# Slot scatters ordered one slot later, from a ring of four output buffers

## The reference

```python
x = x + gnn(layernorm(x), adj)       # quantised weights and activations, relu, adj @ support
xn = layernorm(x)
probs = softmax(xn @ Wr + br); top 2 of 16 experts per row, weights renormalised
h = gelu(layernorm(xn @ W1[e] + b1[e]) * g1[e] + be1[e])
y = x + sum over the row's 2 experts of weight * (h @ W2[e] + b2[e])
```

## Time and profile before

| what | us |
|---|---|
| median of 3 runs | 493.76 |
| the runs | 492.7 to 495.56 |
| the profiled execution | 493.86 |
| its span in the profile | 492.1 |
| PE busy | 454.0 (92%) |
| DVE busy | 350.0 (71%) |
| ACT busy | 306.0 (62%) |
| POOL busy | 228.2 (46%) |

### The profile page before, as it was taken

The page is one execution under the profiler, slowest core; times in us unless marked ns, Lnnn a source line. Parts: engine busy times, 40 slices in busy tenths (PEclk is TensorE's granted clock), DMA queues, the critical chain, the costliest instruction groups (busy, mean ns, idle before and its releaser), DMA issues.

```text
span 492.1 us, 10312 instructions
## 1 busy us (share of the span) xinstructions
PE 454.0 (92%) x2260; PEld 373.2 (76%) x2261; DVE 350.0 (71%) x735; ACT 306.0 (62%) x511; POOL 228.2 (46%) x267
## 2 busy tenths in 40 slices
PE   0789999999999999989999999999899998999990
PEld 0568888877888888868777888888787776888870
DVE  5898864786788877876757686677896775767730
ACT  1667462474544334346878778779886975897550
POOL 4363330342155627553455655454535636455542
PEclk9999999999999999899999999999999999999997
DMA  8621224885645644249969787966889788675543
GB/s 303 266 79 51 87 65 172 297 313 171 227 156 178 206 137 130 85 116 276 282 173 257 210 246 199 252 134 206 258 239 302 234 218 259 164 193 87 87 67 43
DMA packets 33532, 91.30 MB, mean 186 GB/s; under 512 B 6160, under 2 KB 6304, under 8 KB 32992
## 3 DMA queue, kind: packets, MB, share of 16 engines
q1 hardware_dynamic: 19664, 60.60, 37.6%
q0 software_dynamic: 9232, 21.98, 21.0%
q10 hardware_dynamic: 4608, 8.39, 4.6%
HBM read 71.89 MB, written 19.07 MB: 185 GB/s over the span
## 4 chain that ended last, share of the span: by engine, by line
PE 60%; DMA 14%; DVE 8%; issue 6%; ACT 3%; DVEq 2%; POOL 2%; SPq 1%; POOLq 1%; ACTq 1%
PE ps L1595 18%; PE ps L1854 7%; PE ps L1858 7%; PE ps L1850 7%; PE ps L1579 6%; DMA w_raw<-in_w 6%; DMA out<-y_sb,scat_i 5%; PE ps L1567 5%; PE ps L1635 2%; PE ps L1760 2%; PE ps L1874 2%; DVE w_split L1460 1%; PE ps L1626 1%; DMA gw_raw<-in_gnn_w 1%; PE ps L1555 1%
## 5 line engine op out<-in xcount | busy, mean ns | idle before, releaser
L776 POOL DMA_INDIRECT out<-y_sb,scat_i x35 | 63.0, 1799 | 43.2 <-DMA out<-y_sb,scat_i 25.7
L1460 DVE TENSOR_TENSOR w_split<-w_raw,w_split x56 | 67.2, 1221 | 11.1 <-issue 10.4
L747 POOL DMA_INDIRECT xg<-xn_rows,tok_i x39 | 45.4, 1164 | 46.4 <-ACT gate L972 31.7
L1021 ACT ACTIVATE g_sb<-ps,be_sb,g_sb 128x128 f32<-128x128 f32 x152 | 56.9, 455 | 15.8 <-PE ps L1874 15.6
L832 ACT ACTIVATE adj_hi<-adj_raw,small 128x1024 fp32r<-128x1024 f32 x32 | 36.8, 1150 | 40.6 <-PE ps L1595 34.5
L1007 ACT ACTIVATE w_split<-w_raw x28 | 53.0, 1912 | 5.9 <-DMA w_raw<-in_w 4.9
L1153 DVE SCALAR_TENSOR_TENSOR adj_lo<-adj_raw,small,adj_hi 128x1024 fp32r<-128x1024 f32 x32 | 40.8, 1276 | 19.7 <-ACT adj_hi L832 19.6
L1483 DVE TENSOR_SCALAR h_hat<-ps,h_mv,h_rs 128x512 f32<-128x512 f32 x38 | 30.7, 809 | 26.2 <-POOL h_rs L758 26.1
L1595 PE MATMUL ps<-sup,adj_lo 128*128 128x512 f32 x192 | 49.2, 398 | 0.0
L1595 PE MATMUL ps<-sup,adj_hi 128*128 128x512 f32 x192 | 49.2, 398 | 0.0
L1850 PE MATMUL ps<-w_split,gt_hi 128*128 x152 | 44.5, 414 | 0.7 <-ACT gt_hi L1026 0.7
(11 more groups left out here) (220 smaller groups left out, 952.6 us busy)
## 6 DMA issues: line engine op xcount, KB each, us to landing
w_raw<-in_w SPq DMA_DIRECT2D x64, 512.0 KB
adj_raw<-in_adj_steps SPq DMA_DIRECT2D x32, 512.0 KB, 3.5
out<-x_sb ACTq DMA_DIRECT2D x16, 256.0 KB, 2.8
xn_rows<-xn ACTq DMA_DIRECT2D x16, 256.0 KB, 2.8
bias_rows<-in_b SPq DMA_DIRECT2D x16, 256.0 KB
x_sb<-in_x SPq DMA_DIRECT2D x3, 1024.0 KB, 12.3
gw_raw<-in_gnn_w SPq DMA_DIRECT2D x1, 1024.0 KB, 4.9
x_sb<-in_x SPq DMA_DIRECT2D x2, 512.0 KB, 6.7
```

Source lines behind the costliest of these rows:

```text
L747: return pool.indirect_dma_start(to, None, xn_rows, bass.IndirectOffsetOnAxis(ap=tok_i[:, s:s + 1], axis=0)).then_inc(landed[s % 2], 16)
L776: pool.indirect_dma_start(out, bass.IndirectOffsetOnAxis(ap=at, axis=0), y_sb[:, par, :], None, compute_op=ALU.add).then_inc(scattered[par ...
L1021: ins = act.activation(g_sb[:, par, c * P:(c + 1) * P], ht_ps(par)[:, c * P:(c + 1) * P], ACT.Gelu, scale=g1_sb[:, bass.ds(e * C + c, 1)], ...
L1460: return dve.tensor_tensor(w_parts(n, 1, e + 1, 2 * h, 2), w_raw[:, n, :, :].rearrange("p a n -> p (a n)")[:, at], w_parts(n, 0, e + 1, 2 ...
```

## The change

In `pool_pair`, iteration s now orders the scatter of slot s - 2 instead of s - 1. The first scatter moves from ahead of the loop into it. In the last pair that runs (rest == j) one more scatter, of slot 2j, is ordered at the end, so that again three are left for `give_last`. The gated copies go to a ring of four buffers (`y_ring`, slot modulo 4), and those of the last three slots to three buffers of their own (`y_last`), for which ACT waits for no scatter. Both lie in space that the graph layer used before. The dump rows are written by four DMAs instead of two, so that each parity's semaphore begins at 32 instead of 16; all waits on the scatters are renumbered with it. In the loop ACT's wait has the same number as before and so now means the scatter of slot s - 5 instead of s - 3, where s is the slot whose iteration makes the copy of s - 1.

```diff
--- before.py
+++ after.py
@@ -302,12 +302,16 @@
         g_sb = place("g_sb", [P, 2, D], F32)
         gt_hi = place("gt_hi", [P, 2, D], F32R)
         gt_lo = place("gt_lo", [P, 2, D], F32R)
-        y_sb = place("y_sb", [P, 2, D], F32)
         idx_s = place("idx_s", [P, 3], I32)
         h_stats = place("h_stats", [P, 2, 6], F32)
         h_mv = place("h_mv", [P, 2, 2], F32)
         h_rs = place("h_rs", [P, 2, 4], F32)
         assert where[0] <= end_sup
+
+        where[0] = end_sup
+        y_ring = place("y_ring", [P, 4, D], F32)
+        y_last = place("y_last", [P, 3, D], F32)
+        assert where[0] <= w_at
 
         where[0] = raw_at
         hit_row0 = place("hit_row0", [P, 2 * TQ, P], F32R)
@@ -644,9 +648,9 @@
                     pool.memset(bias_row1[:, :].bitcast(F32), 0.0).then_inc(bias_zero, 1)
             pool.wait_ge(tables_in, 16)
 
-            for h in range(2):
-                pool.dma_start(out[N + h * P // 2:N + (h + 1) * P // 2, :], k_sb[h * P // 2:(h + 1) * P // 2, 0:D]
-                               ).then_inc(scattered[h], 16)
+            for h in range(4):
+                pool.dma_start(out[N + h * P // 4:N + (h + 1) * P // 4, :], k_sb[h * P // 4:(h + 1) * P // 4, 0:D]
+                               ).then_inc(scattered[h % 2], 16)
 
             for dst, name in ((tri_r, "tri"), (ones_r, "ones"), (ident_r, "ident"), (first_r, "first_rank"),
                               (word_r, "word_of")):
@@ -771,18 +775,18 @@
                 pool.wait_ge(gate_ok, s + 4)
                 gather(s + 5)
 
-            def add_rows(at, par):
+            def add_rows(at, rows, par):
                 pool.sem_inc(pool_turn, 1)
                 pool.indirect_dma_start(
                     out, bass.IndirectOffsetOnAxis(ap=at, axis=0),
-                    y_sb[:, par, :], None, compute_op=ALU.add).then_inc(scattered[par], 16)
+                    rows, None, compute_op=ALU.add).then_inc(scattered[par], 16)
 
             def give(s, start):
 
-                pool.wait_ge(scattered[s % 2], s // 2 * 16 + 16)
-                pool.wait_ge(scattered[1 - s % 2], start * 16 + (s + 1) // 2 * 16)
+                pool.wait_ge(scattered[s % 2], s // 2 * 16 + 32)
+                pool.wait_ge(scattered[1 - s % 2], start * 16 + ((s + 1) // 2 * 16 + 16))
                 pool.wait_ge(y_ok, s + 3)
-                add_rows(scat_i[:, s:s + 1], s % 2)
+                add_rows(scat_i[:, s:s + 1], y_ring[:, s % 4, :], s % 2)
 
             early_scatter()
             slot_rstd(1, 1)
@@ -790,13 +794,15 @@
             slot_rstd(2, 0)
             fetch(1)
             pool.wait_ge(e_scattered, 16)
-            give(0, 1)
             def pool_pair(j):
-                earlier, word = load_begins(pool, j - 1), load_begins(pool, j)
+                earlier = load_begins(pool, j - 1)
                 for s in (2 * j, 2 * j + 1):
                     slot_rstd(s + 1, (s + 1) % 2)
                     fetch(s)
-                    give(s - 1, (word & 1) if s % 2 else (earlier >> 1))
+                    give(s - 2, (earlier >> (s % 2)) & 1 if j > 1 or s % 2 else 1)
+                if j >= SURE:
+                    with pool.If(rest == j):
+                        give(2 * j, load_begins(pool, j) & 1)
 
             for j in range(1, SURE + 1):
                 pool_pair(j)
@@ -809,10 +815,10 @@
             def give_last(back, done, starts):
 
                 par = (3 - back) % 2
-                pool.wait_ge(scattered[par], done)
-                pool.wait_ge(scattered[1 - par], starts)
+                pool.wait_ge(scattered[par], done + 16)
+                pool.wait_ge(scattered[1 - par], starts + 16)
                 pool.wait_ge(y_ok, rest * 2 + (4 + back))
-                add_rows(idx_s[:, back:back + 1], par)
+                add_rows(idx_s[:, back:back + 1], y_last[:, back, :], par)
 
             pool.tensor_copy(idx_s[:, :], scat_i[:, bass.ds(rest * 2 + 1, 3)]).then_inc(idx_ok, 1)
             earlier, word = load_begins(pool, rest), load_begins(pool, rest + 1)
@@ -993,11 +999,12 @@
             act.activation(tab_sb[:, :, :], table_t_ps, ACT.Copy).then_inc(tab_ok, 1)
             early_hi(1, 1)
 
-            def gated(n, par, landed):
+            def gated(n, par, rows, landed=None):
 
                 act.wait_ge(mm2, n + 1)
-                act.wait_ge(scattered[par], landed)
-                act.activation(y_sb[:, par, :], y_ps(par), ACT.Copy, scale=gate[:, bass.ds(n + 1, 1)]).then_inc(y_ok, 1)
+                if landed is not None:
+                    act.wait_ge(scattered[par], landed)
+                act.activation(rows, y_ps(par), ACT.Copy, scale=gate[:, bass.ds(n + 1, 1)]).then_inc(y_ok, 1)
 
             def split_next(n, e, start):
 
@@ -1031,7 +1038,7 @@
                 act.wait_ge(y_ok, s + 1)
                 act.activation(y_ps(par), bias_rows2[:, bass.ds((e & 3) * D, D)], ACT.Copy).then_inc(y_seeded, 1)
 
-            def slot(s, par, word, landed, last=False):
+            def slot(s, par, word, rows, landed=None, last=False):
 
                 e_s, e_a = expert_in(word, par), expert_in(word, par + 2)
                 slot_seed(s, par, e_s)
@@ -1039,7 +1046,7 @@
                 if not last:
                     slot_x_hi(s + 3, 1 - par)
                     slot_gate(s + 3, 1 - par, expert_in(word, par + 3))
-                gated(s - 1, 1 - par, landed)
+                gated(s - 1, 1 - par, rows, landed)
                 if not last:
                     split_next(0, e_a, starts_in(word, par + 2))
                 split_next(1, e_s, starts_in(word, par))
@@ -1054,11 +1061,12 @@
             slot_gate(3, 1, expert_in(word, 3))
             split_next(0, expert_in(word, 2), starts_in(word, 2))
             split_next(1, expert_in(word, 0), starts_in(word, 0))
-            slot(1, 1, word, 16)
+            slot(1, 1, word, y_ring[:, 0, :])
             def act_pair(j):
                 word = load_plan(act, j)
                 for par in range(2):
-                    slot(j * 2 + par, par, word, j * 16 + 16 * par)
+                    slot(j * 2 + par, par, word, y_ring.rearrange("p a d -> p (a d)")[:, bass.ds(((j * 2 + (par + 3)) & 3) * D, D)],
+                         j * 16 + 16 * par)
 
             with act.Fori(1, SURE + 1) as j:
                 act_pair(j)
@@ -1069,12 +1077,12 @@
                             act_pair(b * 4 + i + (SURE + 1))
             word = load_plan(act, rest + 1)
             for par in range(2):
-                slot(rest * 2 + (2 + par), par, word, rest * 16 + (16 + 16 * par), last=True)
-            gated(rest * 2 + 3, 1, rest * 16 + 32)
+                slot(rest * 2 + (2 + par), par, word, y_last[:, par, :], last=True)
+            gated(rest * 2 + 3, 1, y_last[:, 2, :])
             for par in range(2):
                 act.wait_ge(gathered[par], rest * 16 + 32)
             for i in range(2):
-                act.wait_ge(scattered[i], rest * 16 + 48)
+                act.wait_ge(scattered[i], rest * 16 + 64)
             act.sem_inc(all_landed, 1)
```

## The result

| what | before, us | after, us |
|---|---|---|
| median (20 runs each) | 493.87 | 497.31 |
| the profiled execution | 493.86 | 496.27 |
| its span | 492.1 | 494.5 |
| H(1) to H(5) | 26.47 | 24.63 |
| H(5) to H(36) | 211.24 | 215.43 |

The changed kernel is slower: ratio 1.0059, 95% interval 1.0037 to 1.008. Five of its twenty runs were slow ones (three of 502 to 504 us, one of 1176, one of 1610) and are left out of the ratio; the median of the other fifteen is 496.94.

The account below looks back on a forecast made before the run. PE held 60% of the chain; its five waits for h_hat, behind POOL's late scatters, put 3.8 us on the path. From 493.76: -1.3 - 0.6 - 1.2 + 0.1 + 0.2 = -2.8, so 491.0 us, range 487.6 to 496.2.

Parts of the forecast that it names:

- First slots: Loop's start: scatter 0 goes behind a gather, the power behind it runs sooner, early PE stalls shrink; -1.3 us.
- Ordinary slots: Slots with no late landing: scatter follows the gather, at H + 5.1, 0.4 us off POOL's lateness, which buys nothing.
- Buffers, registers, dump stores: Ring of four on ACT 0, its address instructions 0.1 us, two more dump stores on POOL 0.
- The third stall of the middle: PE idle 1.27 us at 410.30: chain begins up to 1.65 sooner, against a cost of 1.43; -1.2 us.
- The other middle stalls: Two mid-loop PE stalls of 0.48 and 0.6 us: each chain begins 0.4 earlier; -0.6 for both.
- everything else in the middle: Rest of the mid-loop: waits for landings at experts' starts kept as before, no time gained or lost; 0.
- The tail: Last slots: scatter 34 right behind 33 makes slot 37's h_hat 0.2 to 0.9 us late, mostly covered; +0.2.
- scatters land later: Rival: gather and scatter ordered 0.30 apart on one queue, chained landings grow by 1 us; 496.5 us, chance 0.15.
- A median landing above 8: Sign listed as showing the forecast wrong: scatters' median time from order to landing above 8 us, against 7.1 before.

Follow-up runs that it names:

- e10: Changed kernel with ACT's gate copy at the head of its iteration, POOL's gather also waiting for PE's transposes; ratio 0.9954 to the kernel before.
- e1: Changed kernel's buffers, dump stores and registers, but scatters in the order of before; ratio 1.0011 to the kernel before.
- e5: Changed kernel with only an eighth of each weight half loaded from the third expert on; ratio 0.9896 to the kernel before, span 484.5 us.
- e4: Kernel before with only an eighth of each weight half loaded from the third expert on; ratio 0.9877 to the kernel before, span 484.5 us.

## Why the prediction was wrong

The forecast was 491.0 and faster; it is slower, and the median, 497.31 (496.94 over the fifteen), lies above the range, which ended at 496.2.

- **First slots, -1.3: right in the mechanism, its size hidden by chance.** Scatter 0 at 242.72 (forecast 242.7), the power at 245.87 (246.0), scatter 1 at 249.54, sooner than forecast since the landing took 5.9. H(1) to H(5) is 1.8 shorter. Only about 0.5 of it is behind H(3): H(4) had 7.49 and not 6.58 us, as PE waited 0.6 for gathered rows. The rest lies ahead of H(3), 8.06 us from H(2) before and 6.69 after: a wait of 0.9 for such rows that the profiled execution of before had at 237.85. e10, with the new order, has it too (8.11), so it isn't the order that took it away. Nor does the near match of -1.8 with -1.3 prove the term. Where no rows come late behind H(3), as in e10, H(3) to H(5) is 13.16 us, 1.4 less than before: that does bear it out.
- **Ordinary slots: right.** Scatter 26 goes at 422.41, H + 5.13, with 0.30 behind the gather; forecast H + 5.1.
- **Buffers, registers, dump stores, nothing to 0.1: right**, by e1. The stores (62.62, four in 2.26 us) moved L1603's first product from 86.9 to 87.0.
- **The third stall of the middle, -1.2: right that it goes, too small.** Slots 26 to 28 cost 2.4 less, beyond the bound of 1.4: 1.4 is the step to H(27), where the 1.27 stood, the other 1.0 lies in the steps on its two sides.
- **The other middle stalls, -0.6, and everything else in the middle, 0: the step that failed.** "In the middle each chain begins 0.4 us earlier" and "the wait for the previous landing at an expert's start is kept" took every start's wait as before, as if any scatter could have any landing between 4.8 and 10.2 us. The landings aren't spread like that: the longest stand beside the weight loads, above all in the iteration behind a start, where the gate is late as well. The trace of before could have told it, in a list of each scatter's landing with the iteration it stands in and with who waits for it; starts 16 and 28, not waited for then, don't come up in the prediction. The middle measured +4.2 instead of -1.8, 3.3 of it behind start 5 alone.
- **The tail, +0.2 (0 to +1.5): size off, +0.6.** h_hat of slot 37 was late by 0.28, within the forecast 0.2 to 0.9. Of the 0.6 only 0.24 is there when the last scatter is ordered: scatter 33 goes a slot later, and scatter 35 had to wait for its landing. 0.32 is the landing of the last scatter, 5.30 us instead of 4.98, which nothing ties to the change.
- **The rival "scatters land later", 0.15, 496.5: right in sign and nearly in size, wrong in reason.** It wanted a queue slowed by gather and scatter 0.30 apart. The median landing fell from 7.1 to 5.8, and in e5, with the same spacing, that of the even slots is 4.9. What it missed is that a waited-for landing can grow while the median falls. "A median landing above 8", the sign that was to tell it, would not have shown it.

The timeline of the last slots of the changed kernel, for the tail (H(36) = 472.03):

```profile
470.57 1.59 POOL L780 DMA_INDIRECT out<-y_ring,scat_i  x1 [0.30 <-issue]
...
472.46 1.57 POOL L780 DMA_INDIRECT out<-y_ring,scat_i  x1 [0.30 <-issue]
...
474.28 0.57 POOL L762 TENSOR_TENSOR h_rs<-h_rs,k_sb 128x1 f32<-128x1 f32 x1
...
475.75 0.66 PE L1882 MATMUL ps<-k_sb,h_hat 128*128 128x128 f32 x4 [0.28 <-DVE h_hat L1491]
...
477.51 1.64 POOL L780 DMA_INDIRECT out<-y_last,idx_s  x1 [2.66 <-DMA out<-y_ring,scat_i]
...
485.24 1.54 POOL L780 DMA_INDIRECT out<-y_last,idx_s  x1 [0.30 <-issue]
```

Scatter 34 at 472.46 instead of 469.26; 35 is held 2.66 us for the landing of 33 and goes at H + 5.48 (+5.35 before). The last scatter goes 13.21 behind H(36), before 12.97.

## What to carry to other kernels

Before a step is moved by an iteration, list its instances one by one: what runs beside each, how long each takes, and who waits for it. A minimum, median and maximum over all of them hide that the long ones have an address, and a move can hand that address to the one instance that is waited for. When such a move loses, look for what made the step late in its new place; removing that (here one small copy) may turn the loss into a gain that neither edit brings alone.

## What the runs showed of the hardware

- **Accumulating scatters beside weight loads.** In the kernel before the same 256 KB DMA of 128 rows landed 5.2 us after its order (median, at most 6.8) with an eighth of the weights loaded (e4), and 7.1 (at most 10.2) with all of them, 2 MB an expert.
- **POOL's order of a scatter beside DVE's weight split.** It takes 1.57 to 1.6 us alone and 2.5 where it begins 1.07 us before a split ends (270.27, 2.52, beside the split of 268.99 to 271.34); e10's at 268.90, 2.11, begins 0.66 before a piece of the split ends and is 0.5 longer. The Trainium skill, SBUF — State Buffer, "Who interferes with whom", says that a DVE instruction with two SBUF inputs contends with a GpSimd instruction that reads SBUF, and holds, as inferred, that making descriptors isn't among these. The first sentence fits these rows; the second would have the order unchanged at 1.6 and doesn't. The next pieces of the split begin at 270.07 in e10, still within that order, so the 0.5 and the 0.66 needn't belong together. No run here took the split alone away, so that it is the split and not something else at the same moment stays argued.
- **The length of an undisturbed slot isn't a constant.** Before most take 6.58 us; in the changed kernel slots 5 to 17 take 6.61 to 6.68 where nothing stalls, and most later ones 6.58. That is about 0.4 us of the +4.2. It isn't the order: e1, with that of before, has 6.62 nearly throughout, e10, with the new one, 6.58. The granted clock is 1.0 in all of these, no row has a wait, and it stays unexplained.
- **Two stalls that belong to neither order**: 1.2 to 1.9 us, named issue, at H(18), and 0.2 at H(26) in a slot of 7.6 to 8.0, in the kernel before, the changed one and e10 alike. What holds PE there stays open.
